# Masked peaks in one pass, and division on the context rows, in a decoder's second attention

## The chip, the cores and the metric

The kernel runs on one core of a Trainium2 chip. Its time is the device time of one execution in microseconds (us); the figure for a kernel is the median of several executions. A core has a matrix engine (TensorE, PE in the profile; its weight loads are a row of their own, PEld), VectorE (DVE), ScalarE (ACT) and GpSimd (POOL), each with its own instruction stream, and SyncE, which issues the DMA transfers here. The engines wait for each other by semaphores.

## What is computed

A decoder of two post-norm layers over 8 sequences of 100 rows and width 256. Layer 0 is a diagonal state-space layer, a cross attention to 361 context rows, and a mixture of experts. Layer 1 is a stack of four Mamba layers, a masked cross attention to the same context, and a gated feed-forward with fake-quantised weights and activations. Between the parts stand residual sums and layer norms. The change is in the masked cross attention and in what runs beside it:

```python
def _L1_xattn_ref(q, k, v, mask, Wq, bq, Wk, bk, Wv, bv, Wo, bo):
    bs, sq, _ = q.shape
...
    scores = jnp.einsum('bhqd,bhkd->bhqk', qh, kh) / math.sqrt(D_K)
    scores = jnp.where(mask == 0, -jnp.inf, scores)
    attn = jax.nn.softmax(scores, axis=-1)
    attn = jnp.nan_to_num(attn, nan=0.0)
    x = jnp.einsum('bhqk,bhkd->bhqd', attn, vh)
    x = x.transpose(0, 2, 1, 3).reshape(bs, sq, HIDDEN)
    return x @ Wo + bo

def _weight_fake_quant(w):
    scale = jnp.max(jnp.abs(w), axis=1, keepdims=True) / QMAX
    return jnp.clip(_ste_round(w / scale), -QMAX - 1.0, QMAX) * scale

```

q, k and v are projected and split into 16 heads of 16. The mask is one table per sequence of 100 x 361, shared by the 16 heads. Its last columns are zero, up to 90 of them.

## The kernel before

The first layer runs to about 355 us, the Mamba layers to about 1058, the second attention to about 1258, the feed-forward to the end. Each engine's stream is written out by a function of its own, and the order in it is the order of the calls; nothing is scheduled at build time.

The second attention goes by steps g, one for each head of each sequence (16 per sequence), and by quads n of four heads: quads 0 to 31 are the work, four per sequence, called q0 to q3 below. The table AT says at which step of the 16 each other piece of work stands. `pre(g, at)` names the sequence ahead of the one whose scores run, `fin(g, at)` the one behind it, `ended(g, name)` the same with an earlier step for the last sequence.

TensorE (`pe_attn_last`) does this for each quad n: four scores, 100 x 361 each, one in each of PSUM banks 0 to 3; four more matmuls that add the mask into the same banks (the bf16 identity times `a.mb`, which holds -1e30 where the mask is 0; line 720); the values of quad n-2 (`pe_values`, into bank 4); then the pieces by AT; then the transposes of quad n-1's probabilities, 12 matmuls in three products T0 to T2 (`pe_probs`). The pieces are K0 in q0 and K1 in q1 (keys of the next sequence), V0 in q1, V1 in q2, V2 and the query product Q0, Q1 in q3, the turned query rows XT and the output product O of the sequence before in q2, and the turned result FT in q0. All these and T0 to T2 take turns in PSUM banks 5 to 7: a product waits until the engine that reads the third one before it has freed its bank. The scores of n+1 wait for all four exponentials of n (`exp_ready`), since they write the same banks.

VectorE (`dve_attn`, `dve_quad_last`) at the start of quad n takes the reciprocals of the four sums of n-1 (line 1143), then two reductions over two banks each for the peaks of n, negated (line 1148, `max_ready`). Behind these stand, by steps, the mask of the next sequence (`dve_mask`, four operations), its query rows and their norm's start, V and Q reads from PSUM with the bias (`dve_v`, `dve_q`), the residual sum behind O, and the ends of two norms per sequence (`norm_end`, line 645). Between steps 19 and 83 it also quantises the feed-forward's weights in nine parts (`quantise_weight`): for each of three weights the scales, then two halves of rounding.

ScalarE (`act_attn_last`) does the four exponentials of n from PSUM (line 911), with the peak as bias and the sum from the accumulator, then the copies of K (line 904), XT, FT and of the context (`cT`, line 998), then the copies of T0 to T2 (line 921).

GpSimd (`pool_attn`) multiplies the four exponentials of n-1, in SBUF and in place, by the reciprocal of the sum and by a flag `anyv` that is 0 for a row with nothing unmasked (`pool_scale`, line 1032, `prob_ready`); the transposes wait for that. Its other work there is the middle of the norms (`norm_root`, six small operations) and a residual sum.

Semaphores count up; a function that ends in `then_inc(a.x)` releases who waits for `x`.

## Time and profile before

| | us |
|---|---|
| runs | 1315.11, 1311.96, 1315.26 |
| median | 1315.11 |
| profiled execution | 1320.03 |
| span of its instructions | 1317.9 |
| granted clock of TensorE, mean | 0.941 |
| busy in the span: PE, DVE, POOL, ACT | 1151.7, 1070.4, 833.9, 827.9 |
| second attention, first peak to last residual sum | 1059.35 to 1257.90 |

The rows further down are of three kinds. A timeline row has the start in us from the span's start, the length in us from the first start to the last end, the engine, the line, the operation, what it writes and reads with the matrices' or tiles' shapes, how many instructions stand in the row (a run of equal ones is one row), and in brackets how long the engine had stood idle before it and which engine's work, on which name and line, released it. As ends of matmuls are modelled, the length of a matmul row reaches a little into the next; the distance from start to start is the better measure. A row of a line gives the count and the least, median and greatest length in ns. A row of the page's groups has busy us and mean ns, then idle time ahead and its releaser. A row of stretches has the two ends of the stretch, its length, busy time of PE, PEld, DVE, ACT and POOL with the number of instructions, the granted clock of TensorE (1.00 is 2.4 GHz, 0.50 is 1.2 GHz), the DMA share and GB/s.

### The profile page before, as it was taken

Reading aid. Unit: us, or ns where it says so; the run is one execution under the profiler, and the core shown is the slowest. Engines: PE = TensorE matmul, PEld = TensorE weight load, DVE = VectorE, ACT = ScalarE, POOL = GpSimd, SP = SyncE. Lnnn points to the kernel's source line nnn. Section 1 sums busy time; section 2 is a strip of 40 time slices with the busy share of each in tenths; the row PEclk is TensorE's granted clock in tenths of the full one; section 3 lists DMA queues with packets and bytes.
Section 4 is the critical chain, followed back from the end, with each engine's and each line's share of the span. In section 5 each row is a group of like instructions: output and inputs, shape, how many; then the busy total and the mean of one; then the engine's idle time right before and its main releaser. Section 6 shows DMA issues by size and latency. Waiting matters only on the chain.

```text
span 1317.9 us, 17582 instructions
## 1 busy us (share of the span) xinstructions
PE 1151.7 (87%) x6026; PEld 672.5 (51%) x6026; DVE 1070.4 (81%) x1522; ACT 827.9 (63%) x1827; POOL 833.9 (63%) x743
## 2 busy tenths in 40 slices
PE   7798899878768998999989989899897798899874
PEld 3455555544334554544545545446454466566544
DVE  4577777675689999999999999999999948776556
ACT  1455555664386777766867776767674346667664
POOL 6001111100498998998989989989899736666505
PEclk9899999988889999998999999989998899999975
DMA  6000002000510603206004032050150030010000
GB/s 207 12 12 13 12 13 72 1 1 3 199 40 2 243 1 114 103 1 221 24 19 182 17 140 105 1 201 17 45 187 0 0 97 18 17 33 1 1 1 25
DMA packets 22141, 79.14 MB, mean 60 GB/s; under 512 B 4935, under 2 KB 8847, under 8 KB 21138
## 3 DMA queue, kind: packets, MB, share of 16 engines
q1 hardware_dynamic: 22054, 78.02, 17.1%
q8 instruction: 49, 0.80, 0.3%
q14 instruction: 38, 0.31, 0.1%
HBM read 76.77 MB, written 1.24 MB: 59 GB/s over the span
## 4 chain that ended last, share of the span: by engine, by line
PE 36%; DVE 31%; POOL 14%; ACT 11%; issue 6%; DMA 1%; SPq 0%; ACTq 0%; DVEq 0%; POOLq 0%
PE ps L659 33%; DVE ps L2016 10%; POOL arena L1930 9%; DVE arena L2021 4%; DVE arena L2019 4%; DVE hstat L1148 4%; ACT arena L911 3%; POOL arena L1942 3%; PE ps L733 3%; ACT ps L1813 2%; DVE arena L1979 2%; ACT L654 1%; DVE arena L1136 1%; DMA arena<-in_exb 1%; DVE arena L2311 1%
## 5 line engine op out<-in xcount | busy, mean ns | idle before, releaser
L659 PE MATMUL ps<-arena 128*32 128x100 f32 (+8 forms) x3300 | 520.6, 382 | 70.0 <-ACT arena L911 15.4
L1930 POOL TENSOR_TENSOR arena<-arena 128x1600 f32<-128x1600 f32 x128 | 456.3, 3578 | 34.7 <-DVE ps L2016 26.4
L659 PE MATMUL ps<-arena,ident 128*128 128x400 f32 x1024 | 384.6, 526 | 29.8 <-POOL arena L1942 20.3
L659 PEld LDWEIGHTS ps<-arena 128*32 128x32 f32 (+6 forms) x3300 | 261.8, 146 | 286.3 <-issue 106.0
L1813 ACT ACTIVATE ps<-arena 128x400 f32<-128x400 f32 x512 | 282.9, 589 | 184.5 <-DVE arena L2019 151.2
L2016 DVE TENSOR_TENSOR_SCAN ps<-ps,arena 128x800 f32<-128x800 f32 x176 | 320.6, 1822 | 22.1 <-ACT ps L1813 16.4
L659 PEld LDWEIGHTS ps<-arena,ident 128*128 128x128 f32 x1024 | 201.0, 199 | 196.6 <-issue 28.3
L632 POOL TENSOR_SCALAR stat<-stat 100x1 f32<-100x1 f32 (+1 forms) x44 | 8.6, 196 | 337.5 <-DVE stat L613 336.8
L911 ACT ACTIVATE arena<-ps,hstat 100x361 f32<-100x361 f32 x256 | 141.9, 562 | 101.2 <-DVE hstat L1148 101.1
L2019 DVE TENSOR_TENSOR arena<-ps,arena 128x800 f32<-128x800 f32 x176 | 174.5, 991 | 6.0
L1148 DVE TENSOR_REDUCE hstat<-ps 100x2 f32<-100x722 f32 x128 | 112.8, 903 | 71.1 <-PE ps L659 70.7
L1942 POOL TENSOR_TENSOR arena<-arena 128x1600 f32<-128x1600 f32 x40 | 142.9, 3572 | 16.2 <-DVE arena L2021 16.0
L2021 DVE TENSOR_TENSOR_SCAN arena<-ps,arena 128x800 f32<-128x800 f32 x80 | 140.4, 1804 | 1.0 <-ACT ps L1813 0.8
L733 PE MATMUL ps<-ident,arena 100*128 100x100 f32 x768 | 97.2, 261 | 21.7 <-ACT arena L904 12.3
L921 ACT ACTIVATE arena<-ps 128x400 f32<-128x400 f32 x192 | 92.9, 509 | 27.6 <-PE ps L733 26.8
L733 PEld LDWEIGHTS ps<-ident,arena 100*128 100x128 f32 x768 | 78.4, 145 | 43.8 <-ACT arena L904 14.6
L1032 POOL TENSOR_SCALAR arena<-arena,hstat,anyv 100x361 f32<-100x361 f32 x128 | 81.7, 654 | 20.3 <-DVE hstat L1143 20.3
L654 ACT ACT_TABLE_LOAD x65 | 83.4, 1283 | 1.2
L659 PE MATMUL ps<-wv,arena 128*128 128x256 f32 (+1 forms) x192 | 54.0, 408 | 4.0 <-DVE arena L1116 3.2
L911 ACT ACTIVATION_READ_ACCUMULATOR arena<-ps,hstat 100x1 f32 x256 | 51.9, 203 | 0.0
L659 PE MATMUL ps<-arena,wk 128*128 128x361 f32 x128 | 49.3, 512 | 1.5 <-ACT xm L1695 0.8
L1136 DVE TENSOR_SCALAR arena<-arena,hstat 100x361 f32<-100x361 f32 x128 | 46.5, 406 | 2.3
(191 smaller groups left out, 981.4 us busy)
## 6 DMA issues: line engine op xcount, KB each, us to landing
arena<-bc_scratch SPq DMA_DIRECT2D x64, 800.0 KB, 6.3
arena<-in_ctxT SPq DMA_DIRECT2D x16, 361.0 KB, 3.7
arena<-in_w_in SPq DMA_DIRECT2D x4, 1024.0 KB, 5.0
arena<-in_expT SPq DMA_DIRECT2D x1, 2048.0 KB, 12.8
arena<-in_w_out SPq DMA_DIRECT2D x4, 512.0 KB, 3.2
arena<-in_mask SPq DMA_DIRECT2D x8, 141.0 KB
arena<-in_xT SPq DMA_DIRECT2D x2, 400.0 KB, 4.3
x_tok<-in_x_tok SPq DMA_DIRECT2D x1, 800.0 KB
```

Source lines behind the costliest of these rows:

```text
L654: act.add_instruction(mybir.InstLoadActFuncSet(name=nc.get_next_instruction_name(), act_func_set_id=which, engine=mybir.EngineType.Activat ...
L659: return nc.tensor.matmul(outp, lhsT, rhs, start=first, stop=last)
L733: last = nc.tensor.transpose(ps[:, a.bank(b, name), k * S:(k + 1) * S], a.es[0:S, (n * QUAD + i) % 8, kc * P:(kc + 1) * P], ident[0:S, 0:S])
L911: nc.scalar.activation(a.es[0:S, v % 8, 0:SK], ps[0:S, i, 0:SK], ACT.Exp, bias=hstat[0:S, n % 2, 0, i:i + 1], scale=1.0, accum_out=hstat[0 ...
L921: nc.scalar.activation(a.aT[:, n % 2, r * QUAD * S:(r + 1) * QUAD * S], ps[:, a.bank(b, name), 0:QUAD * S], ACT.Copy).then_inc(a.freed(b, ...
L1148: nc.vector.tensor_reduce(hstat[0:S, n % 2, 0, i:i + 2], ps[0:S, i:i + 2, 0:SK], AX.X, ALU.max, negate=True).then_inc(a.max_ready, 1)
L1813: last = nc.scalar.activation(psf[:, half_at(k) + j * GT:half_at(k) + (j + 1) * GT], delta[g][:, c], ACT.Exp, scale=aneg[:, l % 2, n:n + 1])
L1930: nc.gpsimd.tensor_tensor(bx[:, unit % BX].rearrange("p (j t) -> p j t", j=SEGMENT), bbc[:, nq].rearrange("p (j t) -> p j t", j=SEGMENT), ...
L1942: nc.gpsimd.tensor_tensor(h, h, cbc[:, nq], ALU.mult).then_inc(m_cmp, 1)
L2016: nc.vector.tensor_tensor_scan(a, a, bx[:, unit % BX, w], 0.0, ALU.mult, ALU.add).then_inc(m_scan, 1)
L2019: nc.vector.tensor_tensor(y, a, cbc[:, nq, w], ALU.mult).then_inc(m_cmd, 1)
L2021: nc.vector.tensor_tensor_scan(y, a, bx[:, unit % BX, w], 0.0, ALU.mult, ALU.add).then_inc(m_scan, 1)
```

## The change

Only the second attention and what lies beside it change.

Mask: the four mask matmuls of a quad and the tile `mb` go. `dve_mask` is one operation, which makes `vm`, -1e30 where the mask is 0. The peaks (`dve_masked`) are four fused operations, one per head: each reads the scores from PSUM and `vm`, writes -(score + mask), cut at 1e29, into `es` in SBUF, and gives the least of it, the negated peak. The exponentials (`act_exp_last`) then work in place in SBUF, with scale -1. The scores of n+1 wait for `max_ready` of n, the peaks, and no longer for the exponentials.

Division: the exponentials go undivided into the transposes and the values. Their sums, 16 per sequence, gather in `rsum`. Once per sequence, in the first quad of the next one, VectorE cuts them at 0.5 from below (where nothing is unmasked the sum is 0) and takes reciprocals, each spread to the 16 columns of its head (`dve_inverse`, 100 x 256). TensorE turns these by the identity (`pe_spread`, product RS), ScalarE copies them, and VectorE multiplies the context by them (`dve_context`), in place of ScalarE's copy of it. `pool_scale` goes.

Order on ScalarE: exponentials 0 to 2, then the copies of K, XT and FT, then exponential 3, the copy of RS, and T0 to T2.

Weights: VectorE keeps the scales (`weight_scale`, at steps 19, 43, 67); rounding moves to GpSimd in 18 pieces, one every fourth step from 23 (`quantise_piece`).

Norms: the ends of the second attention's norms move to GpSimd (`norm_end_pool`), the second one straight into `x_tok`, so that VectorE's copy into it goes. Two functions on VectorE wait for these ends.

```diff
+    "1R": 3,
+    "1S": 0,
+    "1C": 4,
...
+        PEAKS_AT = (H + 3, 2 * H + 11, 4 * H + 3)
+        PIECES_AT = range(H + 7, H + 7 + 18 * QUAD, QUAD)
...
+        def norm_end_pool(pool, par, z, dst, done):
+
+            pool.wait_ge(n_root, norms.rooted)
+            st = stat[0:S, par]
+            nc.gpsimd.tensor_scalar(dst, z, st[:, 6:7], st[:, 9:10], ALU.subtract, ALU.mult).then_inc(done, 1)
...
                 for name in ("K1", "Q0", "Q1"):
                     a.wait_read(pe, b, name)
-                if a.layer == 1:
-                    pe.wait_ge(a.mask_ready, b + 1)
             if a.layer == 1 and n == 0:
                 pe.wait_ge(m_scan, 2 * UNITS * ROUNDS)
                 wait_c(pe, UNITS * ROUNDS - 1)
-            wait(pe, a.exp_ready, n * QUAD)
+            wait(pe, a.exp_ready if a.layer == 0 else a.max_ready, n * QUAD)
             for i in range(QUAD):
                 r = slice(32 * i, 32 * i + 32)
-                last = mm(ps[0:S, i, 0:SK], a.qm[r, par, qd], a.kT[r, par, qd // 2], True, a.layer == 0)
-            if a.layer == 0:
-                last.then_inc(a.s_full, 1)
-                return
-            for i in range(QUAD):
-                last = mm(ps[0:S, i, 0:SK], identb[0:S, 0:S], a.mb[0:S, par, 0:SK], False, True)
-                if i % 2:
-                    last.then_inc(a.s_full, 1)
+                last = mm(ps[0:S, i, 0:SK], a.qm[r, par, qd], a.kT[r, par, qd // 2], True, True)
+            last.then_inc(a.s_full, 1)
 
         def pe_probs(pe, a, n, r):
...
             for k in range(QUAD):
                 i, kc = divmod(r * QUAD + k, KC)
                 if k == 0 or kc == 0:
-                    pe.wait_ge(a.prob_ready[i // 2], 2 * n + i % 2 + 1)
+                    if a.layer == 0:
+                        pe.wait_ge(a.prob_ready[i // 2], 2 * n + i % 2 + 1)
+                    else:
+                        pe.wait_ge(a.exp_ready, n * QUAD + i + 1)
                 last = nc.tensor.transpose(ps[:, a.bank(b, name), k * S:(k + 1) * S],
                                            a.es[0:S, (n * QUAD + i) % 8, kc * P:(kc + 1) * P], ident[0:S, 0:S])
...
+        def pe_spread(pe, a, b):
+
+            pe.wait_ge(a.rs_ready, b + 1)
+            a.wait_free(pe, b, "RS")
+            for c in range(KD):
+                last = mm(ps[:, a.bank(b, "RS"), c * S:(c + 1) * S], a.inv[0:S, c * P:(c + 1) * P], ident[0:S, 0:S],
+                          True, True)
+            last.then_inc(a.prod_full, 1)
...
-                        pe_turn(pe, a, b, "FT", a.x2[0:S, b % 2])
+                        pe_turn(pe, a, b, "FT", x_tok[:, b, :])
+                    for b in fin(g, AT["1R"]):
+                        pe_spread(pe, a, b)
...
+        def act_exp_last(act, a, v):
+
+            n, i = divmod(v, QUAD)
+            act.wait_ge(a.max_ready, v + 1)
+            e = a.es[0:S, v % 8, 0:SK]
+            nc.scalar.activation(e, e, ACT.Exp, bias=hstat[0:S, n % 2, 0, i:i + 1], scale=-1.0,
+                                 accum_out=rsum[0:S, n // QUADS % 2, sum_at(n, i)]).then_inc(a.exp_ready, 1)
...
+                for g in quad_steps(n)[:3]:
+                    if has_head(g):
+                        act_exp_last(act, a, g)
                 for g in quad_steps(n):
-                    if has_head(g):
-                        act_exp(act, a, g)
-                for g in quad_steps(n):
-                    for b in fin(g, AT["C"]):
-                        act.wait_ge(a.av_full, (b + 1) * QUADS)
-                        w = QUADS // a.share * S
-                        nc.scalar.activation(a.cT[:, b % 2, 0:w], ps[:, 4, 0:w], ACT.Copy).then_inc(a.cT_ready, 1)
...
+                if has_head(QUAD * n + 3):
+                    act_exp_last(act, a, QUAD * n + 3)
+                for g in quad_steps(n):
+                    for b in fin(g, AT["1R"]):
+                        a.wait_full(act, b, "RS")
+                        nc.scalar.activation(a.cT[:, b % 2, KD * S:2 * KD * S], ps[:, a.bank(b, "RS"), 0:KD * S],
+                                             ACT.Copy).then_inc(a.freed(b, "RS"), 1)
...
-        def pool_scale(pool, a, n):
-
-            pool.wait_ge(a.rs_ready, n + 1)
-            bp = n // QUADS % 2
-            for j in range(QUAD):
-                e = a.es[0:S, (n * QUAD + j) % 8, 0:SK]
-                rs = hstat[0:S, n % 2, 2, j:j + 1]
-                ready = a.prob_ready[j // 2]
-                nc.gpsimd.tensor_scalar(e, e, rs, anyv[0:S, bp:bp + 1], ALU.mult, ALU.mult).then_inc(ready, 1)
...
                     for b in pre(g, AT["1x"]):
                         norm_root(pool, b % 2)
+                        norm_end_pool(pool, b % 2, a.x1[0:S, b % 2], a.x1[0:S, b % 2], a.in_ready)
                     for b in pre(g, AT["1xe"]):
                         gp_residual(pool, a, b)
                     for b in ended(g, "1N"):
                         norm_root(pool, b % 2)
+                        norm_end_pool(pool, b % 2, a.zt[0:S, b % 2], x_tok[:, b, :], a.x_ready)
+                    if g in PIECES_AT:
+                        quantise_piece(pool, PIECES_AT.index(g))
...
-        def dve_sums_last(dve, a, n):
-
-            dve.wait_ge(a.exp_ready, n * QUAD + QUAD)
-            st = hstat[0:S, n % 2]
-            nc.vector.reciprocal(st[:, 2, 0:QUAD], st[:, 1, 0:QUAD]).then_inc(a.rs_ready, 1)
+        def dve_masked(dve, a, n):
+
+            b = n // QUADS
+            if n % QUADS == 0:
+                dve.wait_ge(a.mask_ready, b + 1)
+            dve.wait_ge(a.s_full, n + 1)
+            for i in range(QUAD):
+                nc.vector.tensor_tensor_reduce(
+                    a.es[0:S, (n * QUAD + i) % 8, 0:SK], ps[0:S, i, 0:SK], a.vm[0:S, b % 2], -1.0, LOWEST, ALU.add,
+                    ALU.min, hstat[0:S, n % 2, 0, i:i + 1]).then_inc(a.max_ready, 1)
+
+        def dve_inverse(dve, a, b):
+
+            dve.wait_ge(a.exp_ready, H * (b + 1))
+            sums = rsum[0:S, b % 2]
+            step(nc.vector.tensor_scalar(sums, sums, 0.5, None, ALU.max))
+            nc.vector.reciprocal(a.inv[0:S, :].rearrange("p (h d) -> p h d", h=H),
+                                 sums.rearrange("p (h o) -> p h o", o=1).to_broadcast([S, H, DK])).then_inc(a.rs_ready, 1)
+
+        def dve_context(dve, a, b):
+
+            dve.wait_ge(a.av_full, (b + 1) * QUADS)
+            a.wait_read(dve, b, "RS")
+            w = KD * S
+            nc.vector.tensor_tensor(a.cT[:, b % 2, 0:w], ps[:, 4, 0:w], a.cT[:, b % 2, w:2 * w],
+                                    ALU.mult).then_inc(a.cT_ready, 1)
...
+            if a.layer == 1:
+                dve.wait_ge(a.in_ready, min(b + 3, B))
+                wait(dve, a.x_ready, b - 1)
...
+            wait(dve, a.in_ready, b - 1)
+            wait(dve, a.x_ready, b - 3)
...
-                elif g % QUAD == 0:
-                    dve_quad_last(dve, a, g // QUAD)
+                elif g % QUAD == 0 and has_quad(g // QUAD):
+                    dve_masked(dve, a, g // QUAD)
                 if a.layer == 1:
+                    for b in fin(g, AT["1S"]):
+                        dve_inverse(dve, a, b)
+                    for b in fin(g, AT["1C"]):
+                        dve_context(dve, a, b)
...
-            vstep.mark(nc.vector.tensor_scalar(v, a.mk[0:S, par], 0.0, None, ALU.is_equal))
-            vstep.settle()
-            vstep.mark(nc.vector.tensor_reduce(anyv[0:S, 2 + par:3 + par], v, AX.X, ALU.min))
-            vstep.settle()
-            vstep.mark(nc.vector.tensor_scalar(anyv[0:S, par:par + 1], anyv[0:S, 2 + par:3 + par], -1.0, 1.0,
-                                               ALU.mult, ALU.add))
-            nc.vector.tensor_scalar(a.mb[0:S, par, 0:SK], v, MASKED, None, ALU.mult).then_inc(a.mask_ready, 1)
-            dve.wait_ge(a.mask_ready, b + 1)
+            nc.vector.tensor_scalar(a.vm[0:S, par], a.mk[0:S, par], 0.0, MASKED, ALU.is_equal,
+                                    ALU.mult).then_inc(a.mask_ready, 1)
...
+        def quantise_piece(pool, k):
+
+            G_ = nc.gpsimd
+            w, k = divmod(k, 6)
+            half, pass_ = divmod(k, 3)
+            f, q, _, inv, n = weights[w]
+            h = slice(half * n // 2, (half + 1) * n // 2)
+            if pass_ == 0:
+                pool.wait_ge(f_scaled, w + 1)
+                for c in range(half * n // 2, (half + 1) * n // 2):
+                    last = G_.tensor_scalar(f[:, c], f[:, c], inv[:, c:c + 1], ROUND, ALU.mult, ALU.add)
+                last.then_inc(f_round, 1)
+            elif pass_ == 1:
+                pool.wait_ge(f_round, 2 * w + half + 1)
+                G_.tensor_scalar(f[:, h], f[:, h], ROUND + QMAX, ROUND - QMAX - 1, ALU.min, ALU.max).then_inc(f_clamp, 1)
+            else:
+                pool.wait_ge(f_clamp, 2 * w + half + 1)
+                G_.tensor_scalar(q[:, h], f[:, h], -ROUND, 1.0, ALU.add, ALU.mult).then_inc(f_wq, 1)
```

TensorE in the first quad of a sequence, before: scores wait for the exponentials, the mask matmuls (`identb`) follow; values (32x100), a K product (`wk`), FT (line 775), then the transposes T (line 733).

```order
L659 MATMUL ps<-arena 100x361 [waits a1_mask_ready,a1_free1,a1_exp_ready,a1_free0]
L659 MATMUL ps<-arena 100x361 x3
L659 MATMUL ps<-arena,identb 100x361 x4
L659 MATMUL ps<-arena 32x100 [waits a1_free1,a1_free0,a1_free2]
L659 MATMUL ps<-arena 32x100 x11
L659 MATMUL ps<-arena,wk 128x361 [waits a1_free2,a1_ctx_in1]
L659 MATMUL ps<-arena,wk 128x361
L775 MATMUL ps<-ident,arena 128x100 [waits a1_free0,a1_x_ready]
L775 MATMUL ps<-ident,arena 128x100
L733 MATMUL ps<-ident,arena 128x100 [waits a1_prob_ready0,a1_free1]
L733 MATMUL ps<-ident,arena 128x100 x2
```

The same place after (`ident,arena` at line 672 is RS, line 741 the transposes T):

```order
L672 MATMUL ps<-arena 100x361 [waits a1_free2,a1_max_ready,a1_free1]
L672 MATMUL ps<-arena 100x361 x3
L672 MATMUL ps<-arena 32x100 [waits a1_free2,a1_free1,a1_free0]
L672 MATMUL ps<-arena 32x100 x11
L672 MATMUL ps<-arena,wk 128x361 [waits a1_free0,a1_ctx_in1]
L672 MATMUL ps<-arena,wk 128x361
L792 MATMUL ps<-ident,x_tok 128x100 [waits a1_free1,a1_x_ready]
L792 MATMUL ps<-ident,x_tok 128x100
L672 MATMUL ps<-ident,arena 128x100 [waits a1_free2,a1_rs_ready]
L672 MATMUL ps<-ident,arena 128x100
L741 MATMUL ps<-ident,arena 128x100 [waits a1_exp_ready,a1_free0]
L741 MATMUL ps<-ident,arena 128x100 x2
```

The mask matmuls are gone, the scores wait for the peaks, and two matmuls that wait for `rs_ready` stand between FT and the transposes.

VectorE at the same place, before, in the quad in which the weights' first scales are taken: the sums' reciprocals, the peaks, the mask of the next sequence, its query rows (line 1232) and their norm, the weights' peaks (line 2260).

```order
L1143 RECIPROCAL hstat<-hstat 100x4 [waits a1_exp_ready]
L1148 TENSOR_REDUCE hstat<-ps 100x2 [waits a1_s_full] x2
L2100 TENSOR_SCALAR arena<-arena 100x361 [waits a1_prob_ready1,a1_prob_ready0,a1_ctx_in0]
L2102 TENSOR_REDUCE anyv<-arena 100x1 [waits dve_steps]
L2104 TENSOR_SCALAR anyv<-anyv 100x1 [waits dve_steps]
L2106 TENSOR_SCALAR arena<-arena 100x361
L1232 TENSOR_TENSOR arena<-x_tok,xm 100x256 [waits m_free6,xo2,a1_mask_ready]
L611 BN_STATS stat<-arena 100x6 [waits dve_steps]
L612 MEMSET held 1x1 [waits dve_steps]
L613 BN_AGGR stat<-stat 100x2
L2260 TENSOR_REDUCE arena<-arena 88x8 [waits ld_ffn]
```

After, from the last of the four fused operations (line 1174, each followed by its read of the accumulator, `ISA hstat 100x1`):

```order
L1174 ISA arena,hstat<-ps,arena 100x361
L1174 ISA hstat 100x1
L1182 TENSOR_SCALAR rsum<-rsum 100x16 [waits a1_exp_ready]
L1183 RECIPROCAL arena<-rsum 100x256 [waits dve_steps]
L2144 TENSOR_SCALAR arena<-arena 100x361 [waits a1_ctx_in0]
L1276 TENSOR_TENSOR arena<-x_tok,xm 100x256 [waits xo2,m_free6]
L618 BN_STATS stat<-arena 100x6 [waits a1_in_ready,dve_steps]
L619 MEMSET held 1x1 [waits dve_steps]
L620 BN_AGGR stat<-stat 100x2
L2298 TENSOR_REDUCE arena<-arena 88x8 [waits ld_ffn]
```

The small reciprocal of each quad is gone; behind the peaks of a sequence's first quad stand the clamp and the wide reciprocal, and the mask is one operation.

## Rows read from the trace of the kernel before

**Rows 1.** Stretches of the trace, the second attention's stage.

```profile
1058.00:1250.00 192.00, 173.10 (x1766) 117.22 (x1766) 124.08 (x286) 124.85 (x387) 111.52 (x216) 0.99 0.11 29
```

**Rows 2.** Timeline of TensorE over the sequence of quads 24 to 27.

```profile
1205.97 0.87 PE L659 MATMUL ps<-arena 32*100 32x361 f32 x8
1206.77 0.82 PE L659 MATMUL ps<-arena,identb 100*100 100x361 bf16 x4
1207.52 0.72 PE L659 MATMUL ps<-arena 128*32 128x100 f32 x24
1208.17 1.48 PE L659 MATMUL ps<-arena,wk 128*128 128x361 f32 x4
1209.49 0.34 PE L775 MATMUL ps<-ident,arena 100*128 100x100 f32 x2
...
1211.05 0.91 PE L733 MATMUL ps<-ident,arena 100*128 100x100 f32 x8 [0.88 <-ACT arena L904]
1211.89 0.87 PE L659 MATMUL ps<-arena 32*100 32x361 f32 x8
...
1217.19 0.91 PE L733 MATMUL ps<-ident,arena 100*128 100x100 f32 x8 [0.42 <-ACT arena L904]
1218.03 0.87 PE L659 MATMUL ps<-arena 32*100 32x361 f32 x8
...
1221.34 1.05 PE L659 MATMUL ps<-wv,arena 128*128 128x256 f32 x4
1222.23 1.56 PE L733 MATMUL ps<-ident,arena 100*128 100x100 f32 x12
1223.72 0.87 PE L659 MATMUL ps<-arena 32*100 32x361 f32 x8
...
1229.04 0.87 PE L659 MATMUL ps<-arena 32*100 32x361 f32 x8
```

**Rows 3.** Timeline of ScalarE in quad 24.

```profile
1208.26 0.56 ACT L911 ACTIVATE arena<-ps,hstat 100x361 f32<-100x361 f32 x1 [1.62 <-DVE hstat L1148]
1208.72 0.19 ACT L911 ACTIVATION_READ_ACCUMULATOR arena<-ps,hstat 100x1 f32 x1
1208.81 0.56 ACT L911 ACTIVATE arena<-ps,hstat 100x361 f32<-100x361 f32 x1
```

**Rows 4.** Timeline of VectorE, the peaks of quads 4, 28 and 31.

```profile
1087.33 1.73 DVE L1148 TENSOR_REDUCE hstat<-ps 100x2 f32<-100x722 f32 x2 [1.75 <-PE ps L659]
...
1230.38 1.73 DVE L1148 TENSOR_REDUCE hstat<-ps 100x2 f32<-100x722 f32 x2 [1.82 <-PE ps L659]
...
1245.96 1.73 DVE L1148 TENSOR_REDUCE hstat<-ps 100x2 f32<-100x722 f32 x2 [0.75 <-PE ps L659]
```

**Rows 5.** One line's lengths (first row), and groups of the page (the others).

```profile
L2037 DVE TENSOR_TENSOR arena<-ps,arena x32: 561/564/575, 390.1 to 1058.0; 128x400 f32<-128x400 f32 x32
...
L2016 DVE TENSOR_TENSOR_SCAN ps<-ps,arena 128x800 f32<-128x800 f32 x176 | 320.6, 1822 | 22.1 <-ACT ps L1813 16.4
...
L1032 POOL TENSOR_SCALAR arena<-arena,hstat,anyv 100x361 f32<-100x361 f32 x128 | 81.7, 654 | 20.3 <-DVE hstat L1143 20.3
```

**Rows 6.** Lengths of the two lines with reciprocals of 4 and 8 columns.

```profile
L1143 DVE RECIPROCAL hstat<-hstat x32: 144/172/180, 1063.4 to 1249.2; 100x4 f32<-100x4 f32 x32
...
L2262 DVE RECIPROCAL arena<-arena x3: 166/199/200, 1093.9 to 1166.3; 88x8 f32<-88x8 f32 x2, 128x2 f32<-128x2 f32 x1
```

**Rows 7.** Lengths of the weights' peak reductions.

```profile
L2260 DVE TENSOR_REDUCE arena<-arena x3: 1587/2248/2272, 1091.4 to 1164.5; 88x8 f32<-88x2048 f32 x2, 128x2 f32<-128x1408 f32 x1
```

**Rows 8.** Two stands of TensorE on its timeline, and the stretches behind them.

```profile
1122.36 0.82 PE L733 MATMUL ps<-ident,arena 100*128 100x100 f32 x7 [1.60 <-ACT arena L904]
...
1122.30:1127.00 4.70, 4.64 (x53) 3.24 (x54) 2.15 (x4) 2.82 (x9) 2.60 (x5) 1.00 0.00 0
...
1233.89 0.31 PE L733 MATMUL ps<-ident,arena 100*128 100x100 f32 x1 [1.58 <-ACT arena L1010]
...
1233.50:1238.00 4.50, 4.11 (x40) 2.23 (x40) 1.46 (x3) 1.86 (x7) 2.52 (x4) 0.62 0.00 0
```

74 lines of the change are left out of this document (29 added, 45 removed).

## The prediction

> **What bounds the kernel now.** I read first the table of stretches, for the stage that the change touches (1058 to 1258 us). TensorE is busy 173.1 of 192 us there, GpSimd 111.5, VectorE 124.1, ScalarE 124.9, at a granted clock of 0.99 [rows 1]. So TensorE is the frame, and what counts is its matmul time and the moments at which it stands. The timeline of TensorE over one sequence of four quads shows these (q0 from 1205.97 to 1211.89, then q1, q2, q3 to 1229.04) [rows 2]. From one start to the next: scores 0.80, mask matmuls 0.75, values 0.65, one K key product 1.32, a V product 0.89. Eight transposes of probabilities take 0.84 (1211.05 to 1211.89), so the twelve of a quad, T below, take about 1.3. TensorE waits in two places, 0.88 in q0 and 0.42 in q1, both for ScalarE's copy of K, which stands behind four exponentials in ScalarE's order [rows 2, 3]. With these, q0 comes to 0.80 + 0.75 + 0.65 + 1.32 + 0.17 (two FT transposes) + 1.3 + 0.88 = 5.9 and q1 to 6.1; measured are 5.92, 6.14, 5.69 and 5.32, in sum 23.07.
>
> The timeline of VectorE gives the whole: the peaks of n=4 start at 1087.33, of n=28 at 1230.38, so six sequences take 143.05 [rows 4]. Six times 23.07 are 138.4; the other 4.6 are, by my reading, sequences in which VectorE also quantises weights.
>
> **The change, part by part.** All is counted against the profiled execution, 1320.03 us; the median of the runs is 1315.11, 4.9 lower, and I move the result by the same.
>
> Mask matmuls: 4 per quad leave, 0.75 each quad, all on TensorE's path. That alone is 3.0 per sequence.
>
> Peaks: two reductions become four fused operations, which read the scores from PSUM, write the masked, negated scores to SBUF and give the minimum, each followed by a read of the accumulator. No row shows this operation. Bounds: VectorE's two-input operation from PSUM takes 0.564 for 400 elements, of which I estimate 0.52 for 361 and 0.45 from start to start; a read of an accumulator costs 0.19 on ScalarE, where it mostly overlaps the next operation [rows 3, 5]. So 0.45 to 0.73 per head; I take 0.56, nearer to the two-input row, since the pairs on ScalarE (exponential 0.56, read, next exponential 0.55 after the first) hide the read. The first starts 0.98 after the scores do, the fourth ends at 3.22. A worse bound is the scan over two inputs, 1822 ns for 800 elements, 2.3 ns each [rows 5], which would be 0.9 per head.
>
> Waits: scores of n+1 now wait for the four peaks of n, not its exponentials, so ScalarE's exponentials leave TensorE's loop. But with K and the other copies ahead of the fourth exponential and the T transposes still behind, the quads are laid out again, from their pieces: q1 4.97 (pieces back to back: 0.80+0.65+1.32+0.89+1.31), q2 its 5.69 less the mask, 4.94, and 0.20 more wait for VectorE's read of the O and V banks, which now stands behind the fourth peak (3.22 and some 0.45), 5.14; q3 its 5.32 less the mask, 4.57, and 0.44 wait for the same, 5.01.
>
> Division: GpSimd's 4 multiplications per quad at 0.654 [rows 5] leave. They fall away under cover, except behind the last quad. In their place, once per sequence, VectorE clamps the 16 sums and takes a reciprocal of them spread to 256 columns; TensorE multiplies it by the identity (RS); ScalarE copies it; VectorE multiplies the context by it instead of ScalarE's copy. The reciprocal takes 172 ns on 4 columns and 199 on 8 [rows 6]: 6.8 ns a column over those, or 0.199 + 248 × 0.0068 = 1.9 us for 256. This is a long reach from two short rows, so the bounds are wide: were the difference mostly something else, 1.04 ns an element, half the scan's price [rows 5], would give 0.42. I take 2.0, since the rate is what the only reciprocal rows show.
> The Trainium skill, VectorE: DVE Perf Modes, section "First, the fixed hardware budget", says that a reciprocal is an iterative divide with a repeat count of 8. With the 0.96 GHz of the page, 256 columns would then be some 2.1 us (an estimate); the trace agrees, with its 6.8 ns a column. By it the short reciprocal below would fall away and the sum would stand as it is.
>
> What that does to q0: the peaks of q0 end at 3.22 and the clamp at 3.44, since VectorE's order has them first; the reciprocal ends at 5.44. TensorE has scores, values, K and FT (2.94) and then RS, which **waits for the reciprocal and stands ahead of the T transposes**, although these are ready. RS is at 5.5 to 5.93 (two products of 100 rows in fp32, four records at 0.105), T to 7.24. So q0 becomes 7.24, against 5.92: 1.32 worse, where the mask matmuls and the wait for K should have made it 1.6 better. The sequence is 7.24 + 4.97 + 5.14 + 5.01 = 22.36, against 23.07.
>
> Weights: the peak reductions of 2.27, 2.27 and 1.6 us [rows 7] stay on VectorE, the rest goes to GpSimd, whose 4 × 0.654 per quad are free for it. Of the reductions I count 3.7 in all, since VectorE's four peaks (2.24 against 1.70) leave no slack for them. That the rest leaves VectorE is in the six 22.36.
>
> Clock: TensorE will now stand about 2.5 us in each q0. In this trace it stood 1.58 before 1233.89, and the clock granted from 1233.5 to 1238 was 0.62, where 4.11 us of matmuls would have taken 2.55 at full clock; at 1122.36 it stood 1.60, and the clock there stayed at 1.00 [rows 8]. So a stand of 2.5 seems likely, not sure, to cost. I take three in four at 1.4 us (1.56, less a little that hides in waits), 1.05 per sequence, 6.3 in six. This is the softest term: 0 to 9.
>
> Ends: quads 0 to 3 have no RS. They lose the mask (3.0) and 0.5 of waits for K, and gain 0.7 of new waits: −2.8. Quads 28 to 31 take 15.6 from peak to peak now [rows 4]; q0 there has no K product and stands longer, +1.7 with its clock, and the next two are bounded by peaks, then exponentials and scores, and lose some 0.6 each: +0.5. Behind quad 31, GpSimd's 2.6 and the small reciprocal leave, and 2.2 for clamp and reciprocal, 0.43 for RS and the T transposes behind it come; exponentials end 0.7 earlier: 0. Norm ends on GpSimd and the copies that leave VectorE lie beside other work: 0, else 0.3 at the last one. The feed-forward stage is untouched.
>
> Sum: six sequences 134.2 + 3.7 + 6.3 = 144.2 against 143.05, +1.1; ends −2.8 + 0.5 + 0 = −2.3. In all **−1.2**: 1318.8 profiled, 1313.9 in the runs. I say 1314.
>
> **The rivals.** A is this sum, with its own range 1309 to 1321 (clock term 0 to 9, peaks 0.50 to 0.62).
> B, the stand doesn't hurt. Either the reciprocal is short (0.42), q0 loses 1.58 in seven sequences and no clock falls: 1314 − 11.1 − 6.3 = 1297; or it takes 1.5 us and the clock holds: 1314 − 3.5 − 6.3 = 1304. For it: one of two stands in the trace left the clock alone, and most of the cost hangs on a rate from 4 and 8 columns. Against: that rate is steep.
> C, slower: VectorE's fused peaks are dear, **and VectorE becomes the bound**. At 0.73 per head the fourth peak ends 0.68 later; that moves q0's reciprocal, q2's and q3's reads by 0.68, 2.0 per sequence, 13 to 14 in all: 1328. At the scan's 2.3 ns an element four take 3.3 to 3.7 us per quad, and the loop scores, peaks, scores with VectorE's reads is longer than TensorE's pieces in all four: some 37 more, 1351. It decides from about 0.62 per head, where the time crosses 1319. For it: nothing in the trace prices this operation. Against: the plain two-input row from PSUM.
> D, the change doesn't take effect as written: masked quads aren't freed, because T transposes of n−1 still wait for exponentials of n−1 that the copies on ScalarE delay, or GpSimd's pieces delay its norms: 1316 to 1325, with the mask's gain used up.
>
> **How the numbers follow.** A 0.42, B 0.30, C 0.20 (0.14 at 1328, 0.06 far above), D 0.08. A measurement of this kernel tells some 0.3% from no change, 3.9 us: faster is below 1311.2, slower above 1319.1. A gives 0.06 faster, 0.25 same, 0.11 slower; B 0.30 faster; C 0.20 slower; D 0.02 faster or same, 0.06 slower, rounded to 0.37, 0.26 and 0.37. A's own range holds most of the same; over all, 1300 to 1330 leaves out the shortest form of B and the dearest of C, some 2 in 10. It is wide, as the reciprocal's length, the fused operation's price and the clock's answer are each unmeasured.
>
> **What would show it.** In the trace after: RECIPROCAL 100x256 at 1.9 to 2.1 us (0.4 is B); a pitch of 0.5 to 0.6 us of the fused peaks (0.7 or more is C); TensorE idle some 2.5 us before the first spread product of each sequence, and T right behind it; a lower granted clock after most of these; quads q1 to q3 at about 5.0; 22.4 us a sequence without clock loss. The prediction is wrong if RS is not what TensorE waits for, or if q1 to q3 don't shrink by 0.3 to 1.2 each.

## Result, and the profile after

The changed kernel takes 1300.8 us (median of 4 runs, 1297.96 to 1304.22), the kernel before, beside it, 1314.86. The ratio is 0.9881, with a 95% interval from 0.9846 to 0.9915: faster by 1.2%, 14 us. The forecast was 1314, no change. The time lies inside the given range of 1300 to 1330, but no change was forecast, and the measured gain is clear of zero.

The stage's own lengths say where it went. They are from the profiled executions (1320.03 us before, 1300.62 after); the part ahead of the stage, which the change doesn't touch, ended 6.8 us earlier in the second one, and over all traces of this study it ended anywhere between 1046 and 1062 us, so only distances inside the stage are compared.

| from peak to peak | before | after | difference | forecast |
|---|---|---|---|---|
| quads 0 to 4 | 27.98 | 25.11 | -2.9 | -2.8 |
| quads 4 to 28, six sequences | 143.05 | 132.31 | -10.7 | +1.1 |
| quads 28 to 31 | 15.58 | 16.12 | +0.5 | +0.5 |
| quad 31 to the last residual sum | 11.94 | 12.57 | +0.6 | 0 |

In these executions nearly all of the error is in the six middle sequences: 132.3 where the forecast had 144.2. This is the timeline of VectorE in quad 24, a first quad, without the accumulator reads behind the first two peaks; it answers to [rows 4] and to the operations that [rows 5, 6] bound:

```profile
1186.26 0.54 DVE L1174 CUSTOM_DVE_ANT_0 arena<-ps,arena 100x361 f32<-100x361 f32 x1 [1.59 <-PE ps L672]
...
1186.72 0.53 DVE L1174 CUSTOM_DVE_ANT_0 arena<-ps,arena 100x361 f32<-100x361 f32 x1
...
1187.18 0.53 DVE L1174 CUSTOM_DVE_ANT_0 arena<-ps,arena 100x361 f32<-100x361 f32 x1
1187.63 0.08 DVE L1174 DVE_READ_ACCUMULATOR2_ANT hstat<- 100x1 f32 x1
1187.63 0.53 DVE L1174 CUSTOM_DVE_ANT_0 arena<-ps,arena 100x361 f32<-100x361 f32 x1
1188.09 0.08 DVE L1174 DVE_READ_ACCUMULATOR2_ANT hstat<- 100x1 f32 x1
1188.09 0.17 DVE L1182 TENSOR_SCALAR rsum<-rsum 100x16 f32<-100x16 f32 x1
1188.29 1.75 DVE L1183 RECIPROCAL arena<-rsum 100x256 f32<-100x256 f32 x1
```

The fused peak takes 0.53, but from start to start only 0.455: the read of the accumulator starts together with the next peak and costs nothing. The wide reciprocal takes 1.75, not 2.0. The timeline of TensorE for quads 24 to 27 answers to [rows 2]:

```profile
1185.22 1.54 PE L672 MATMUL ps<-arena 32*100 32x361 f32 x32
1186.69 1.48 PE L672 MATMUL ps<-arena,wk 128*128 128x361 f32 x4
1188.01 0.34 PE L792 MATMUL ps<-ident,x_tok 100*128 100x100 f32 x2
1190.10 0.89 PE L672 MATMUL ps<-ident,arena 100*128 100x100 f32 x4 [1.76 <-DVE arena L1183]
1190.78 2.21 PE L741 MATMUL ps<-ident,arena 100*128 100x100 f32 x12
1192.92 2.70 PE L672 MATMUL ps<-arena 32*100 32x361 f32 x32
1195.55 2.32 PE L672 MATMUL ps<-arena,wk 128*128 128x361 f32 x4
1197.70 1.03 PE L672 MATMUL ps<-wv,arena 128*128 128x256 f32 x4
1198.56 1.25 PE L741 MATMUL ps<-ident,arena 100*128 100x100 f32 x12
1199.74 1.60 PE L672 MATMUL ps<-arena 32*100 32x361 f32 x32
1201.27 1.11 PE L672 MATMUL ps<-wo,arena 128*100 128x256 f32 x4
1202.21 0.34 PE L792 MATMUL ps<-ident,arena 100*128 100x100 f32 x2
1202.39 1.05 PE L672 MATMUL ps<-wv,arena 128*128 128x256 f32 x4
1203.27 1.25 PE L741 MATMUL ps<-ident,arena 100*128 100x100 f32 x12
1204.45 1.53 PE L672 MATMUL ps<-arena 32*100 32x361 f32 x32
```

Scores and values are one row now, as the mask matmuls between them are gone. TensorE stands 1.76 for the reciprocal, ahead of RS and of the transposes behind it. What follows runs slowly: transposes 2.14 from start to start against 1.18 later, the K product 2.15 against 1.32. From 1199.74 on, the third quad goes through without a wait, in 4.71. The stretches show the granted clock of TensorE, 1.00 ahead of the products, 0.62 on the mean of the next 9 us, and 1.00 again:

```profile
1187.00:1190.00 3.00, 1.34 (x6) 0.67 (x4) 2.97 (x9) 2.93 (x10) 0.00 (x0) 1.00 0.00 0
1190.00:1199.00 9.00, 8.90 (x62) 6.38 (x63) 3.93 (x17) 4.79 (x13) 3.48 (x8) 0.62 0.01 4
1199.00:1204.00 5.00, 4.99 (x60) 3.73 (x58) 3.34 (x14) 4.08 (x14) 0.24 (x2) 1.00 0.00 0
```

### The profile page after: what moved, and what is told of

Same layout as the page of the kernel before. It is cut to its first block, busy times and chain, and to the rows that moved or that the text cites. A ratio compares the mean times of both kernels' runs of the same rounds, so it can differ in the third digit from the quotient of the medians.

```text
span 1298.9 us, 17433 instructions
## 1 busy us (share of the span) xinstructions
PE 1133.0 (87%) x5930; PEld 665.4 (51%) x5930; DVE 1060.2 (82%) x1629; ACT 831.1 (64%) x1827; POOL 785.5 (60%) x660
## 4 chain that ended last, share of the span: by engine, by line
PE 40%; DVE 33%; POOL 11%; ACT 9%; issue 7%; DMA 0%; ACTq 0%; SPq 0%; DVEq 0%; POOLq 0%
PE ps L672 36%; DVE ps L2064 10%; POOL arena L1978 6%; DVE arena L2069 5%; DVE arena L2067 4%; PE ps L741 4%; POOL arena L1990 2%; DVE hstat L1197 2%; ACT ps L1861 2%; DVE arena L2027 2%; DVE arena L1174 1%; ACT L667 1%; ACT arena L930 1%; DVE arena L1164 1%; ACT arena L945 1%
## 5 line engine op out<-in xcount | busy, mean ns | idle before, releaser
L672 PE MATMUL ps<-arena 128*32 128x100 f32 (+8 forms) x3300 | 521.0, 386 | 71.4 <-ACT arena L930 14.8
L954 ACT ACTIVATE arena<-ps 128x400 f32<-128x400 f32 x192 | 90.1, 502 | 23.3 <-PE ps L741 22.2
L945 ACT ACTIVATE arena<-arena,hstat 100x361 f32<-100x361 f32 x128 | 74.9, 588 | 39.0 <-DVE hstat L1174 39.0
L1174 DVE CUSTOM_DVE_ANT_0 arena<-ps,arena 100x361 f32<-100x361 f32 x128 | 60.6, 530 | 47.7 <-PE ps L672 47.7
L741 PE MATMUL ps<-ident,arena 100*128 100x100 f32 x768 | 93.7, 262 | 5.8 <-DVE arena L1321 2.4
L930 ACT ACTIVATE arena<-ps,hstat 100x361 f32<-100x361 f32 x128 | 71.5, 561 | 36.3 <-DVE hstat L1197 36.2
L1197 DVE TENSOR_REDUCE hstat<-ps 100x2 f32<-100x722 f32 x64 | 57.8, 905 | 26.6 <-PE ps L672 26.2
## 6 DMA issues: line engine op xcount, KB each, us to landing
arena<-in_expT SPq DMA_DIRECT2D x1, 2048.0 KB, 12.5
```

What stands on the lines that cost most here:

```text
L672: return nc.tensor.matmul(outp, lhsT, rhs, start=first, stop=last)
L741: last = nc.tensor.transpose(ps[:, a.bank(b, name), k * S:(k + 1) * S], a.es[0:S, (n * QUAD + i) % 8, kc * P:(kc + 1) * P], ident[0:S, 0:S])
L930: nc.scalar.activation(a.es[0:S, v % 8, 0:SK], ps[0:S, i, 0:SK], ACT.Exp, bias=hstat[0:S, n % 2, 0, i:i + 1], scale=1.0, accum_out=hstat[0 ...
L945: nc.scalar.activation(e, e, ACT.Exp, bias=hstat[0:S, n % 2, 0, i:i + 1], scale=-1.0, accum_out=rsum[0:S, n // QUADS % 2, sum_at(n, i)]).t ...
L954: nc.scalar.activation(a.aT[:, n % 2, r * QUAD * S:(r + 1) * QUAD * S], ps[:, a.bank(b, name), 0:QUAD * S], ACT.Copy).then_inc(a.freed(b, ...
```

## The experiments

Lengths of quads below are distances between the first peaks of neighbouring quads, in us, q0 to q3 of a sequence that holds no weight reduction and no slow clock unless said. The kernel before was run beside each set; its medians there were 1313.2, 1315.5 and 1315.9. "The middle" is quads 4 to 28. It comes, as all lengths here, from one profiled execution for each kernel, which need not be the one at the median: that of peaks alone took 1289.5, 11 below its median, and that of the reciprocal of 16 columns 1290.6, 4.7 above. How often the clock falls in the middle also differs between executions, by 3 to 4 us for kernels that are nearly the same (132.3 for the changed kernel, 128.9 with the memsets). So the columns q0 to q3 say more than the middle, and the middle more than a single time.

| kernel | median | ratio to before (95%) | middle | q0 | q1 | q2 | q3 |
|---|---|---|---|---|---|---|---|
| changed | 1300.8 | 0.988 (0.985 to 0.992) | 132.3 | 6.42 | 4.87 | 4.72 | 4.57 |
| TensorE kept busy | 1293.6 | 0.983 (0.980 to 0.987) | 126.3 | 6.41 | 4.87 | 4.72 | 4.57 |
| reciprocal of 16 columns | 1285.9 | 0.978 (0.974 to 0.982) | 119.8 | 5.37 | 4.81 | 4.79 | 4.57 |
| RS in the second quad | 1294.9 | 0.984 (0.980 to 0.987) | 127.8 | 5.24 | 5.46 | 4.71 | 4.56 |
| both of these | 1289.9 | 0.982 (0.977 to 0.986) | 121.5 | 4.69 | 5.69 | 4.71 | 4.56 |
| 16 columns, RS behind T | 1289.2 | 0.980 (0.977 to 0.983) | 121.2 | 5.73 | 4.80 | 4.79 | 4.57 |
| memsets behind the peaks, pitch 0.474 | 1300.2 | 0.988 (0.984 to 0.992) | 128.9 | 6.48 | 4.87 | 4.78 | 4.58 |
| pitch of peaks 0.567 | 1312.9 | 0.999 (0.997 to 1.000) | 141.1 | 6.85 | 4.87 | 5.15 | 4.95 |
| pitch of peaks 0.737 | 1332.1 | 1.013 (1.010 to 1.015) | 154.2 | 7.53 | 5.11 | 5.83 | 5.64 |
| scores wait for exponentials | 1305.1 | 0.992 (0.991 to 0.994) | 128.2 | 6.42 | 4.87 | 4.72 | 4.56 |
| division per quad | 1304.5 | 0.992 (0.990 to 0.994) | 136.4 | 4.70 | 5.75 | 4.72 | 5.26 |
| rounding on VectorE | 1307.1 | 0.993 (0.990 to 0.996) | 132.9 | 6.41 | 4.87 | 4.80 | 4.57 |
| peaks alone | 1300.7 | 0.987 (0.982 to 0.992) | 130.9 | 4.70 | 5.78 | 4.71 | 5.28 |

### The pitch of the peaks

The pitch is the distance from the start of one fused peak to the start of the next. My first theory was that the 0.56 per head, taken in place of a measured price, made the whole error. The first try puts two memsets of one element behind each peak:

```diff
                     ALU.min, hstat[0:S, n % 2, 0, i:i + 1]).then_inc(a.max_ready, 1)
+                for _ in range(2):
+                    nc.vector.memset(pad[0:1, (n % 4 * QUAD + i) * 2 + _:(n % 4 * QUAD + i) * 2 + _ + 1], 0.0)
```

> The changed kernel with two memsets of one element on VectorE behind each fused peak, to bring its pitch from 0.455 to about the 0.56 that the prediction took. Theory A, that the prediction's error is this pitch: the fourth peak ends 0.42 later, the first quads grow by 0.4 and the third and fourth by the waits of 0.2 and 0.44 that the layout had, in sum some 1.0 per sequence and 6 to 8 us over all, 1307 to 1309. Theory B, that the layout's waits in the third and fourth quads are themselves wrong, and only the first quads pay: 3 us, 1304.

It took 1300.19 us, as the changed kernel. That says nothing on the theory, as the pitch hardly changed; the timeline of VectorE:

```profile
1186.93 0.54 DVE L1175 CUSTOM_DVE_ANT_0 arena<-ps,arena 100x361 f32<-100x361 f32 x1 [1.60 <-PE ps L673]
...
1187.40 0.53 DVE L1175 CUSTOM_DVE_ANT_0 arena<-ps,arena 100x361 f32<-100x361 f32 x1
1187.41 0.06 DVE L1179 MEMSET pad<- 1x1 f32 x2
...
1187.88 0.52 DVE L1175 CUSTOM_DVE_ANT_0 arena<-ps,arena 100x361 f32<-100x361 f32 x1
```

Two memsets of one element behind an operation of 0.53 are nearly free, some 0.02 for both. The second try adds a reduction over columns of the mask tile, whose result nobody uses:

```diff
                     ALU.min, hstat[0:S, n % 2, 0, i:i + 1]).then_inc(a.max_ready, 1)
+                nc.vector.tensor_reduce(hstat[0:S, n % 2, 3, i:i + 1], a.vm[0:S, b % 2, 0:48], AX.X, ALU.max)
```

> The changed kernel with a reduction over 48 columns of the mask tile on VectorE behind each fused peak (its result is not used): the pitch of the peaks goes from 0.455 to about 0.56, the value that the prediction took. Theory A, the prediction's layout was right for this pitch: third and fourth quads grow from 4.72 and 4.57 to 5.14 and 5.01, the first by 0.4: six middle sequences 1.3 longer each, 1308 to 1310. Theory B, TensorE's pieces still cover the reads of O and V at this pitch (in the changed kernel the O read ends 0.36 ahead of the transpose that needs its bank, and the fourth peak comes 0.42 later): third and fourth quads grow by less than 0.1 each, only the first pays 0.42 in seven sequences: 1304.

> The same with 210 columns: a pitch of about 0.73, the upper bound of the prediction and the place of its rival C (1328 there, slower than the kernel before). By theory B the fourth peak comes 1.1 later; the first quads pay all of it (7.7), third and fourth about 0.7 and 0.6 each in six sequences (8): 1316. By the prediction's layout (theory A) 1.3 + 2.0 more per sequence: 1320 to 1324.

1312.89 us with 48 columns (10 runs) and 1332.1 with 210. The timeline of VectorE in the first, with the pitch, and of TensorE in the same fourth quad (quad 23):

```profile
1197.25 0.53 DVE L1174 CUSTOM_DVE_ANT_0 arena<-ps,arena 100x361 f32<-100x361 f32 x1
...
1197.70 0.20 DVE L1177 TENSOR_REDUCE hstat<-arena 100x1 f32<-100x48 f32 x1
...
1197.82 0.52 DVE L1174 CUSTOM_DVE_ANT_0 arena<-ps,arena 100x361 f32<-100x361 f32 x1
...
1198.94 0.41 DVE L1144 TENSOR_TENSOR arena<-ps,bvb 105x256 f32<-105x256 f32 x1
1199.28 0.75 DVE L1151 SCALAR_TENSOR_TENSOR arena<-ps,bq,head_rows 128x200 f32<-128x200 f32 x2
...
1199.41 1.25 PE L741 MATMUL ps<-ident,arena 100*128 100x100 f32 x12 [0.24 <-DVE arena L1144]
```

At 0.567 per head the third quad is 5.15 and the fourth 4.95; the prediction had 5.14 and 5.01. The wait for the V read behind the peaks is there, 0.24 where 0.44 was laid out, and gone at 0.455. My theory B, that only the first quads pay, falls: it gave 1304. Theory A's 1308 to 1310 is too low; the medians are 12 us apart for 0.11 per head. The traces don't account for all of that. The middle is 8.8 longer, of which 1.26 per sequence are undisturbed quads (21.83 against 20.57), 7.5 in all. From the first peak to the last residual sum, with the ends, it is 6.2 (192.3 against 186.1), and 4.5 of the 10.4 between the two profiled executions lie ahead of the stage, which the edit doesn't touch. So what the pitch is shown to cost is about 7.5 us in undisturbed quads; the remainder of the 12 stays open. The clock over the middle was 0.94, against 0.95 in the changed kernel. At 0.737, the upper bound, the kernel is slower than before, 1332 where the rival C had 1328.

### The clock

Seven products of the identity with itself go ahead of TensorE's wait for the reciprocal; RS overwrites their result:

```diff
+            a.wait_free(pe, b, "RS")
+            for _ in range(7):
+                mm(ps[:, a.bank(b, "RS"), 0:P], ident[:, :], ident[:, :], True, True)
             pe.wait_ge(a.rs_ready, b + 1)
-            a.wait_free(pe, b, "RS")
```

> The changed kernel with seven 128 x 128 fp32 products of the identity (about 1.5 us, their result is overwritten) put on TensorE ahead of its wait for the reciprocal, into RS's own bank. They do nothing for the output. If the falls of the clock behind the stands cost the 6 to 7 us that the quads of the trace suggest (second quads of 6.0 instead of 4.7), this kernel is faster than the changed one by that, 1294, with the clock at 1.00 behind six of seven reciprocals. If the clock's cost is hidden by other waits: same time, 1301. If the products delay RS: slower by 1 to 3.

1293.57 us (1292.2 to 1296.4): 7 less than the changed kernel, as expected, and also less than the kernel with the memsets beside it (1299.6 to 1300.5). Each of the seven products has two records in the trace:

```profile
1186.34 1.75 PE L672 MATMUL ps<-ident 128*128 128x128 f32 x14
1188.26 0.69 PE L672 MATMUL ps<-ident,arena 100*128 100x100 f32 x4 [0.17 <-DVE arena L1185]
```

Over the middle of this kernel and of the changed one, the stretches:

```profile
1079.00:1205.00 126.00, 122.41 (x1378) 90.88 (x1372) 89.94 (x308) 97.53 (x293) 57.45 (x120) 1.00 0.07 18
```

```profile
1078.00:1210.00 132.00, 119.00 (x1291) 84.65 (x1287) 89.79 (x309) 98.37 (x293) 57.44 (x120) 0.95 0.06 17
```

Products that nobody reads make the kernel faster: every quad has the length of the changed kernel's undisturbed ones, and the slow ones, 8.26 and 6.15 behind the stand shown above, or 6.79 and 6.01 in quads 8 and 9, are gone. The falls of the clock cost 6.05 in the middle of that execution of the changed kernel (132.31 less 126.26), three falls behind six stands. That is not the same in every execution: with the memsets, and with the scores' wait below, only two of six stands were followed by one, and the middle holds some 2 us of it (128.9 and 128.1).

### The stand for the reciprocal

The reciprocal is taken of the 16 sums, and a copy spreads it to 256 columns:

```diff
             step(nc.vector.tensor_scalar(sums, sums, 0.5, None, ALU.max))
-            nc.vector.reciprocal(a.inv[0:S, :].rearrange("p (h d) -> p h d", h=H),
-                                 sums.rearrange("p (h o) -> p h o", o=1).to_broadcast([S, H, DK])).then_inc(a.rs_ready, 1)
+            step(nc.vector.reciprocal(sums, sums))
+            nc.vector.tensor_copy(a.inv[0:S, :].rearrange("p (h d) -> p h d", h=H),
+                                  sums.rearrange("p (h o) -> p h o", o=1).to_broadcast([S, H, DK])).then_inc(a.rs_ready, 1)
```

> The changed kernel with the reciprocal taken of 16 columns and a copy that spreads it to 256, in place of the reciprocal of 256 columns. Theory that the length of the wide reciprocal sets the stand: 1.75 us becomes about 0.25 + 0.35, so 1.15 less in each of seven quads, 8 us, and with a stand of 0.6 fewer clock falls, 1 to 6 us more: 1287 to 1292. Rival: the stand is bound by the exponentials of the sequence before or by the clamp's wait, not by the reciprocal: within 2 us of the changed kernel.

1285.92 us, the lowest median of the study, and faster than before (0.978) and than the changed one. VectorE's timeline in quad 28 and TensorE's in quad 24:

```profile
1203.66 0.17 DVE L1182 TENSOR_SCALAR rsum<-rsum 100x16 f32<-100x16 f32 x1
1203.86 0.25 DVE L1183 RECIPROCAL rsum<-rsum 100x16 f32<-100x16 f32 x1
1204.15 0.29 DVE L1184 COPY arena<-rsum 100x256 f32<-100x256 f32 x1
```

```profile
1184.97 0.69 PE L672 MATMUL ps<-ident,arena 100*128 100x100 f32 x4 [0.58 <-DVE arena L1184]
```

0.8 from the clamp's start to the copy's end in place of 1.95. The stand is 0.58 instead of 1.76, each first quad 1.05 shorter, 6.3 in six, and the clock stays at 1.00 over the middle, which is worth 6.0 against that execution of the changed kernel: together 12.3 of the 12.5 us between 132.3 and 119.8.

The next two kernels move RS to the second quad, the first alone and the second with the narrow reciprocal:

```diff
-    "1R": 3,
+    "1R": 4,
...
-    "1C": 4,
+    "1C": 6,
```

> The changed kernel with RS moved from the first quad of a sequence to the second, behind K1 (step 3 to 4), and the multiplication of the context behind the V read (step 4 to 6). Theory: in the changed kernel TensorE stands 1.75 us for the wide reciprocal in each first quad, 3.0 in the last one, and the clock falls after some of these stands. Without them the trace should show no stand before RS, all clocks at 1.00 there, and first quads of about 4.7 instead of 6.4 to 8.3: some 13 us from the stands and up to 6.7 from the clock, 1300.8 to about 1283, not below 1279. Rival: the stand hides ScalarE's copies (four exponentials, K, FT, three T, 4.3 us a quad), which then bound the first quads at 5.5 or more: 1290 to 1296.

> The changed kernel with both edits that helped alone: the reciprocal on 16 columns and a spreading copy, and RS in the second quad. Against the narrow one alone (first and second quads 5.37 and 4.80) the first should lose its stand of 0.7 and RS's 0.5 but meet the wait for ScalarE's copies that the late RS showed (5.24), and the second take RS: 5.1 and 5.2, nothing gained in the middle, some 2 to 3 in the last quads: 1283 to 1287.

1294.85 and 1289.89 us. RS in the second quad takes the stand away, but less comes of it than 13 us: the rival of the first expectation holds (1290 to 1296). TensorE in quad 24 of the first kernel, and the start of quad 25:

```profile
1188.65 0.51 PE L741 MATMUL ps<-ident,arena 100*128 100x100 f32 x4
1189.65 0.91 PE L741 MATMUL ps<-ident,arena 100*128 100x100 f32 x8 [0.50 <-ACT arena L923]
1190.49 0.87 PE L672 MATMUL ps<-arena 32*100 32x361 f32 x8
1191.71 0.72 PE L672 MATMUL ps<-arena 128*32 128x100 f32 x24 [0.36 <-ACT arena L954]
```

Once TensorE no longer stands for VectorE, it stands for ScalarE: 0.50 for the copy of K, which is behind three exponentials, and 0.36 for the transposes' copies. The stand had covered both. Nor are all clocks at 1.00 in this kernel: in quad 5, where VectorE takes a weight's peaks ahead of the attention's, the transposes stand for longer, and the clock over quads 5 and 6 is 0.73 and 0.75:

```profile
1089.33 2.40 PE L741 MATMUL ps<-ident,arena 100*128 100x100 f32 x12 [2.21 <-ACT arena L923]
```

The second kernel has q0 and q1 of 4.69 and 5.69, in sum 10.4, where the narrow reciprocal alone has 10.2.

The last try keeps RS in the first quad and puts it behind the transposes, on TensorE, in the order of banks and on ScalarE:

```diff
-                    for b in fin(g, AT["1R"]):
-                        pe_spread(pe, a, b)
                 if has_quad(n - 1):
                     for r in range(KC):
                         pe_probs(pe, a, n - 1, r)
+                for b in fin(QUAD * n + 3, AT["1R"]):
+                    pe_spread(pe, a, b)
```

> The narrow reciprocal, with RS in the first quad but behind the transposes instead of ahead of them. TensorE's work there is 4.66; with the wait of 0.5 for ScalarE's copy of K about 5.15, against 5.37 of the narrow one alone: 0.2 in six sequences, and about 1.5 in the last first quad, where there is no K: 1282 to 1285. Rival: ScalarE's copies of the transposes, now ahead of RS's copy, hold the context and with it O: 1287 or more.

1289.18 us; the expected 1282 to 1285 was missed. Its q0 is 5.73, not 5.15. The transposes meet the same 0.50 for K's copy, and RS behind them a second wait:

```profile
1182.92 0.51 PE L741 MATMUL ps<-ident,arena 100*128 100x100 f32 x4
1183.92 0.91 PE L741 MATMUL ps<-ident,arena 100*128 100x100 f32 x8 [0.50 <-ACT arena L923]
1185.20 0.66 PE L672 MATMUL ps<-ident,arena 100*128 100x100 f32 x4 [0.38 <-ACT arena L954]
```

RS's 0.52 was in the expected 4.66 and K's wait in the 5.15; most of what was missing is the 0.38 that RS waits for ScalarE's copy of the transposes. Intervals of the last three kernels touch that of the narrow one, and which is the fastest isn't shown. The narrow one has the lowest median and the shortest middle, but the one with RS behind T is shorter in quads 28 to 31 (13.4 against 14.8), and from the first peak to the last residual sum the two profiled executions took 171.9 (narrow) and 170.4 (RS behind T).

### Parts of the change

The first edit puts back the scores' wait for the exponentials:

```diff
-            wait(pe, a.exp_ready if a.layer == 0 else a.max_ready, n * QUAD)
+            wait(pe, a.exp_ready, n * QUAD)
```

> The changed kernel, but the scores of a quad wait for all exponentials of the one before, as in the kernel before, not for its peaks. Theory that this wait was never what ended last in middle quads (the fourth exponential ends some 0.3 before TensorE reaches the next scores): within 2 us of the changed kernel, 1300 to 1303. Rival, that freeing the scores is a large part of the gain: 0.3 to 0.5 per quad, 1308 to 1315.

1305.1 us, which medians don't tell from the changed kernel. The quads do: the four of an undisturbed sequence are the same to 0.01. Only at the stage's start, where nothing else is under way, the wait is seen (first quad 8.20, not 6.36). Its middle is 4 us shorter than the changed kernel's, as two and not three of its stands there were followed by a slow clock (0.97 granted). So letting the scores go ahead of the exponentials brought nothing in the undisturbed quads.

Division per quad: the old scaling on GpSimd, with a clamp, `rs_ready` per quad and ScalarE's copy of the context, and no RS:

```diff
+                if a.layer == 1 and i == 0 and has_quad(n - 1):
+                    pool_scale(pool, a, n - 1)
...
-                    if a.layer == 0:
-                        pe.wait_ge(a.prob_ready[i // 2], 2 * n + i % 2 + 1)
-                    else:
-                        pe.wait_ge(a.exp_ready, n * QUAD + i + 1)
+                    pe.wait_ge(a.prob_ready[i // 2], 2 * n + i % 2 + 1)
```

> One half of the change alone: masked peaks, scores that wait for the peaks, rounding and norm ends on GpSimd as in the changed kernel, but the division by the old way, per quad, the reciprocal of four sums on VectorE and four multiplications on GpSimd ahead of the transposes; no wide reciprocal, no RS, ScalarE copies the context. Theory that the division per sequence costs TensorE's stand and clock and brings nothing that was on the path: first quads of about 5.0, the others as in the changed kernel or 0.3 longer, no clock falls: 1285 to 1292. Rival, that taking GpSimd out of the chain exponentials to transposes is what brings the gain: transposes wait for GpSimd (2.6 us behind the last exponential) in every quad, 0.5 to 1 each: 1305 to 1315.

1304.47 us, between the two theories, next to the rival. The longest quads (seven of 6.2 to 8.2) are among those in which GpSimd also rounds. GpSimd and TensorE in one of them, quad 15:

```profile
1144.34 1.22 POOL L656 TENSOR_SCALAR x_tok<-arena,stat 100x256 f32<-100x256 f32 x1
1145.55 1.84 POOL L2320 TENSOR_SCALAR arena<-arena 88x256 f32<-88x256 f32 x4
1147.36 2.20 POOL L1057 TENSOR_SCALAR arena<-arena,hstat 100x361 f32<-100x361 f32 x4
1149.64 1.04 POOL L2324 TENSOR_SCALAR arena<-arena 88x1024 f32<-88x1024 f32 x1
```

```profile
1148.08 2.02 PE L736 MATMUL ps<-ident,arena 100*128 100x100 f32 x12 [1.59 <-POOL arena L1057]
```

TensorE stands 1.59 for the scaling (line 1057), which stood behind the end of a norm and a piece of rounding (1.84), and then follows it head by head, 1.94 for twelve transposes instead of 1.18. The next run gives the rounding back to VectorE as well, with the old nine parts:

> Masked peaks alone: division per quad through GpSimd and rounding on VectorE, both as in the kernel before; scores wait for peaks, norm ends on GpSimd. In the run with division per quad and rounding on GpSimd, quads in which GpSimd also rounded were 6 to 8 us long, and the sequence after the rounding had 4.70, 5.75, 4.72, 5.26. Theory that the two loads collided on GpSimd: without it six middle sequences of 20.4 plus some 5 for VectorE's reductions and rounding, 127.5 instead of 136.4: 1293 to 1297, faster than the whole change. Rival, that the scaling itself holds the transposes: 1302 to 1306, as that run.

> The changed kernel with the rounding of the weights back on VectorE, in the old nine parts; the three scale reductions stand where they stood. Each of six parts takes about 2.5 us of VectorE in a first or third quad, in which VectorE already has 6.5 or 4.3 us of work behind its peaks' start. Theory that the next peaks then come late: 1.5 to 2.2 for each part, 9 to 13 in all: 1308 to 1313. Rival, that VectorE's idle time takes it in: 1301.

Peaks alone: 1300.74 us, as fast as the whole change, middle 130.9. The middle goes the way of the theory of the collision (136.4 to 130.9), but not down to the expected 127.5, and the median missed the expected 1293 to 1297; the two medians' intervals overlap. So the collision is seen in the trace, and its price is not settled. The second, rounding on VectorE in the otherwise changed kernel, is 1307.13, just under the expected 1308 to 1313. Against undisturbed quads and the reductions' 2.8 its middle holds 6.7 us more. Three falls of the clock are in it, of which the last lengthens quads 20 and 21 by 1.5. So moving the rounding is worth about 5 in undisturbed quads where the division leaves GpSimd free, and by the middles less than nothing where GpSimd still scales; the medians, whose intervals overlap, don't show either. The excess is in first quads of 7.7 instead of 6.4 and third quads of 5.6 to 5.8 instead of 4.7 to 4.9, where VectorE's work reaches to the next peaks without a gap.

## Why the prediction was wrong

The layout was right in the main, and the input that weighed most in it was not. By its own steps:

- **Mask matmuls**: right, gone everywhere; the first four quads gave 2.9 where 2.8 was said.
- **Fused peaks, 0.56 per head**: this is the step that failed. The lower bound, 0.45, was the value. The two-input row gave 0.45 from start to start, and the text took a value above it for the accumulator's read, though the row pair on ScalarE [rows 3] shows such a read overlapped; it even said so. With 0.567 in fact, the kernel has nearly the q2 and q3 of the layout (5.15 and 4.95, for 5.14 and 5.01) and takes 1312.9 us, where the forecast was 1314. Per sequence it is 1.26 us (21.83 less 20.57), 7.5 over the middle, and some 12 in the medians. That the median comes so near the forecast is in part luck, as the other terms below were too high by 4 us and the medians move more than the stage does.
- **Reciprocal, 2.0**: 1.753; the reach from 4 and 8 columns had given 1.9. 0.25 per sequence, 1.5 in the middle. The Trainium skill, VectorE: DVE Perf Modes, section "First, the fixed hardware budget", states a repeat count of 8 for the reciprocal; the estimate of 2.1 us worked out from it is 8.3 ns a column, and the 6.8 of the rows, which the prediction called agreement, lies a fifth below it. The trace has 1.753 for 256 columns and 0.253 for 16, 6.25 ns a column, so the measurement decides for less. The short bound, too, has a slip: half the scan's 2.28 ns is 1.14 and not 1.04, which makes 0.44 of the 0.42; it changes nothing else.
- **Transposes**: 1.18 for twelve, not 1.3. The 1.3 was read behind GpSimd's scaling, which the change removes; with it the transposes of peaks alone took 1.2 to 2.0, but that the scaling made the 1.3 isn't shown. With the rest of the small terms 0.3 per sequence.
- **Waits of the scores**: that they no longer wait for the exponentials brought nothing in undisturbed quads (6.42, 4.87, 4.72 and 4.56 with the old wait).
- **RS ahead of T**: right. TensorE stands 1.7 to 1.9 there, where 2.5 was said, and 3.0 where there is no K product. It was cheaper than said, since the stand covers waits for ScalarE of 0.50 and 0.36; those are seen only when it goes.
- **Weights' reductions, 3.7**: 2.8 (1.1, 1.0 and 0.7 by quads of the busy kernel).
- **Clock, 6.3**: 6.05 in the profiled execution, by three falls behind six stands, where the forecast had three in four. That the softest term came out best is luck: in two executions with the same stands and the pitch of 0.455 to 0.474 it was about 2.
- **Ends, -2.3**: -1.8 (-2.9, +0.5, +0.6).

So the middle was 20.57 × 6 + 2.8 + 6.05 = 132.3, against 22.36 × 6 + 3.7 + 6.3. Of the 11.9 between, 10.7 are in the quads, and 7.5 of these are the pitch. Rival B's price came out near (1297 to 1304), but not by its mechanisms: the reciprocal is long and the clock falls. Rival C was real and close: at 0.737 per head the time is 1332, and by the two doses a line crosses the kernel before at about 0.59 per head. D's price did not come, though its doubt that freeing the scores would help was right. The forecast gave faster and slower the same chance, 0.37 each.

One correction to the description of the change: 1e29 is the start value of the fused operation's minimum and limits the peak alone; what is written to `es` isn't cut. The description itself needs this: with all of `es` at 1e29 in a fully masked row, the exponentials would be 1 and their sum not 0.

## What to carry to other kernels

Take a new operation's cost from start to start of its nearest relative, and ask of each small companion (an accumulator read, a memset) whether the trace shows one that costs anything there. When a term is multiplied by four heads and stands ahead of what several quads wait for, 0.1 us in it can decide the sign (here it turns near 0.59), so say at which value the forecast turns. A value for 16 columns should be computed on 16 and then spread: the reciprocal of 256 columns made each first quad 1.05 us longer and, in the profiled execution, cost as much again by the slow clock behind its stands; and before removing a stand, look at which other waits it hides.

## What was unexpected

A stand of 1.7 us is followed by a slow clock in some cases only (four of the seven first quads in the profiled execution of the changed kernel), with a mean of 0.62 over the 9 us shown above. What decides between them isn't shown. Fourteen records of idle products in the stand keep it at 1.00 and save 7 us. The end of a norm on 100 x 256 takes 1.22 on GpSimd, where VectorE's took 0.41:

```profile
L658 POOL TENSOR_SCALAR x_tok<-arena,stat x8: 1217/1221/1225, 1095.0 to 1241.9; 100x256 f32<-100x256 f32 x8
```

GpSimd is busy for 57.4 of 132 us in the middle; no run moved the norm ends alone, so that they cost nothing there isn't shown. A step of the rounding on 88 x 1024 takes 1.04 on GpSimd, in the row shown above, and 0.69 on VectorE.
